# Second attention: scores by two row tiles of 64 rows with four masked heads each, instead of four row tiles of 32 rows with two

## The reference

```python
# x: 64 images x 64 tokens x 256; H = 16 heads of HD = 16
cq = gelu(x @ wq + bq);  ckv = gelu(x @ wkv + bkv)
q_c = cq @ wqc + bqc;    q_r = rope(x @ wqr + bqr)
k_c = ckv @ wkc + bkc;   k_r = rope(x @ wkr + bkr)
v = ckv @ wv + bv
q = gelu(concat(q_c, q_r));  k = gelu(concat(k_c, k_r))    # 256 columns, split in 16 heads
scores = q @ k.T / sqrt(16), causal, in each image and head
out = softmax(scores) @ v @ wo + bo
```

## Time and profile before

| what | us |
|---|---|
| three timed runs | 1585.34, 1585.96, 1579.11 (median 1585.34) |
| the profiled execution, its own time | 1588.56 |
| its span in the trace | 1586.7 |
| TensorE busy | 1388.1 (87% of the span) |
| VectorE busy | 1047.5 (66%) |
| ScalarE busy | 758.5 (48%) |
| GpSimd busy | 634.1 (40%) |
| mean granted clock of TensorE | 0.926 of full speed |

### The profile page before, as it was taken

The page is one execution under the profiler, slowest core; times in us unless marked ns, Lnnn a source line. Parts: engine busy times, 40 slices in busy tenths (PEclk is TensorE's granted clock), DMA queues, the critical chain, the costliest instruction groups (busy, mean ns, idle before and its releaser), DMA issues. The chain is left out here.

```text
span 1586.7 us, 37038 instructions
## 1 busy us (share of the span) xinstructions
PE 1388.1 (87%) x14188; PEld 1219.2 (77%) x14188; DVE 1047.5 (66%) x2196; ACT 758.5 (48%) x1288; POOL 634.1 (40%) x608
## 2 busy tenths in 40 slices
PE   6979999999999987768994588889976889999995
PEld 5867888888888877768994466667756889999994
DVE  4744674674674675876566567888776876666775
ACT  5433444444444442334553366767742346666641
POOL 4005422112112002535627255333336757663765
PEclk9999999999999998889997788999975899999997
DMA  8304664243353104225865000000008248888963
GB/s 287 119 26 152 220 210 147 88 160 116 105 174 134 55 2 156 103 96 172 250 196 161 6 28 28 2 1 2 2 1 318 104 163 253 266 273 255 280 214 111
DMA packets 142883, 215.57 MB, mean 136 GB/s; under 512 B 14336, under 2 KB 112768, under 8 KB 141824
## 3 DMA queue, kind: packets, MB, share of 16 engines
q1 hardware_dynamic: 121648, 160.20, 30.4%
q0 software_dynamic: 18624, 52.45, 10.5%
q10 hardware_dynamic: 2448, 0.61, 0.2%
HBM read 103.64 MB, written 109.58 MB: 134 GB/s over the span
## 5 line engine op out<-in xcount | busy, mean ns | idle before, releaser
L125 PE MATMUL e_p_gu<-e_w_hi,e_xt_hi 128*128 (+1 forms) x676 | 200.8, 297 | 12.9 <-DVE e_xt_lo L723 9.6
L125 PE MATMUL e_p_gu<-e_w_hi,e_xt_lo 128*128 (+1 forms) x676 | 195.0, 288 | 0.0
L125 PE MATMUL e_p_gu<-e_w_lo,e_xt_hi 128*128 (+1 forms) x676 | 194.9, 288 | 0.0
L125 PEld LDWEIGHTS e_p_gu<-e_w_hi,e_xt_hi 128*128 128x128 f32 x676 | 132.9, 197 | 15.1 <-issue 12.8
L1271 POOL DMA_INDIRECT e_xn<-results,e_row_of x112 | 115.6, 1032 | 62.6 <-issue 28.9
L125 PEld LDWEIGHTS e_p_gu<-e_w_lo,e_xt_hi 128*128 128x128 f32 x676 | 133.3, 197 | 0.0
L125 PEld LDWEIGHTS e_p_gu<-e_w_hi,e_xt_lo 128*128 128x128 f32 x676 | 133.2, 197 | 0.0
L125 PE MATMUL e_p_y<-e_w_hi,e_hid_hi 128*128 (+1 forms) x338 | 110.9, 328 | 8.9 <-DVE e_hid_lo L742 7.0
L1254 POOL DMA_INDIRECT rows<-e_xn,e_row_of x96 | 95.5, 995 | 52.9 <-issue 28.7
L1938 DVE TENSOR_TENSOR a_ot_lo<-a_O,a_ot_hi 128x1024 fp32r<-128x1024 f32 x32 | 39.1, 1223 | 115.3 <-ACT a_ot_hi L1881 115.3
L125 PE MATMUL a_J<-a_xt_hi,w_qk_hi 128*128 128x512 f32 x256 | 106.6, 417 | 8.3 <-DVE a_xt_lo L1956 6.3
(11 more groups left out here) (335 smaller groups left out, 4374.4 us busy)
## 6 DMA issues: line engine op xcount, KB each, us to landing
e_moved<-rows SPq DMA_DIRECT2D x121, 256.0 KB, 3.2
results<-e_y SPq DMA_DIRECT2D x121, 256.0 KB
rows<-a_zero SPq DMA_DIRECT2D x28, 1024.0 KB, 5.8
pa_x<-in_x SPq DMA_DIRECT2D x7, 1536.0 KB, 6.5
w_qk_in<-in_we SPq DMA_DIRECT2D x24, 384.0 KB, 6.3
we_parts<-w_qk_in SPq DMA_DIRECT2D x24, 384.0 KB, 2.5
we_parts<-a_e_lo SPq DMA_DIRECT2D x24, 384.0 KB, 2.4
e_w_hi<-we_parts SPq DMA_DIRECT2D x4, 1536.0 KB, 16.1
```

The source lines that it names most:

```text
L125: mm = eng.matmul(out, lhs[a], rhs[b], start=start and n == 0, stop=stop and n == len(terms) - 1, skip_group_check=skip)
```

## The change

A row tile now covers 64 rows, four heads, and there are two of them, one for each PSUM bank. `kz` holds four masked copies of k instead of two (each with every fourth head), so a matmul streams 4 x 64 = 256 columns. A chunk has 8 matmuls instead of 16. No two row tiles share a bank, so the wait on `row_tile` inside the chunk goes, and one increment per chunk is left. `head_mask` and `kc_bias` have four columns instead of two. ScalarE writes four copies where it wrote two, in both places of `queries_keys`. The place of a head in the scores (`scored`) follows.

```diff
+QUAD = 4
-        kz = [sb(f"kz{i}", [P, KD, IMG_T, 2, SEQ]) for i in range(2)]
+        kz = [sb(f"kz{i}", [P, KD, IMG_T, QUAD, SEQ]) for i in range(2)]
-        scored = lambda b, q: 4 * (q % 2) + 2 * (q // 2) + b
+        scored = lambda b, q: 4 * (q // 2) + 2 * b + q % 2
...
                 act.activation(qt[u][:, 1, :], rope[0][:], ACT.Gelu)
-                for head in range(2):
+                for head in range(QUAD):
                     done = act.activation(kz[u][:, 1, :, head, :], by_image(rope[2][:]), ACT.Gelu, scale=head_mask[:, head:head + 1])
...
                 j.wait_full(act, n, KC)
-                for head in range(2):
+                for head in range(QUAD):
                     done = act.activation(kz[u][:, 0, :, head, :], by_image(p_j[:, 0, :]), ACT.Gelu,
                                           scale=head_mask[:, head:head + 1], bias=kc_bias[:, head:head + 1])
...
-                dve.wait_ge(row_tile, 4 * g + 4)
+                dve.wait_ge(row_tile, g + 1)
...
-                for q in range(4):
-                    rows, bank = slice(32 * q, 32 * q + 32), q % 2
-                    if q >= 2:
-                        pe.wait_ge(row_tile, 4 * g + q - 1)
-                    for b in range(KD):
-                        for i in range(2):
-                            img, at = 2 * c + i, (scored(b, q) % 4) * P
-                            mm = pe.matmul(p_s[SEQ * i:SEQ * (i + 1), bank, at:at + P], qt[u][rows, b, img * SEQ:(img + 1) * SEQ],
+                for b in range(KD):
+                    for i in range(2):
+                        img = 2 * c + i
+                        for bank in range(2):
+                            rows = slice(64 * bank, 64 * bank + 64)
+                            mm = pe.matmul(p_s[SEQ * i:SEQ * (i + 1), bank, b * QUAD * SEQ:(b + 1) * QUAD * SEQ],
+                                           qt[u][rows, b, img * SEQ:(img + 1) * SEQ],
                                            kz[u][rows, b, img].rearrange("p a k -> p (a k)"), start=False, stop=True, skip_group_check=True)
-                    mm.then_inc(row_tile, 1)
+                mm.then_inc(row_tile, 1)
```

More of the change, by code:

```diff
@@ L2171, in attention1_phase @@
         st = sb("st", [P, CH, DVE_BN])
-        cos, sin, head_mask = sb("cos", [P, SEQ]), sb("sin", [P, SEQ]), sb("head_mask", [P, 2])
+        cos, sin, head_mask = sb("cos", [P, SEQ]), sb("sin", [P, SEQ]), sb("head_mask", [P, QUAD])
         bias = sb("bias", [P, 9])
-        kc_bias = sb("kc_bias", [P, 2])
+        kc_bias = sb("kc_bias", [P, QUAD])
         bo = sb("bo", [P, D])
@@ L2716, in pack_attention1 @@
     cos, sin = rope_tables()
-    odd = (np.arange(P) // DK1) % 2
+    place = (np.arange(P) // DK1) % QUAD
     return dict(wa1=np.ascontiguousarray(flat.reshape(P, 4, 1024).transpose(1, 0, 2)), bias1=np.ascontiguousarray(bias),
                 bo=w["bo"].reshape(1, D), cos=cos, sin=sin,
-                head_mask=np.stack([1 - odd, odd], axis=1).astype(np.float32))
+                head_mask=np.stack([place == head for head in range(QUAD)], axis=1).astype(np.float32))
 def combine1(c, entry):
```

## The result

The changed kernel takes 1598.35 us (median of four runs, 1596.19 to 1599.04) against 1582.49 us before in the same runs: a ratio of 1.0103, 95% interval [1.0074, 1.0133], or about 16 us slower. Forecast were 13.6 us more, and 1599 us for the whole. The profiled execution took 1596.19 us, with a span of 1594.3 us.

The account below looks back on a forecast made before the run. A ring of waits through all engines was taken as the bound. Delays of 14.8 us, less 3.7 for score blocks, plus 2.5 for the clock, gave 13.6 us more: 1599 us from a 1585.34 us median, range 1588 to 1610.

Parts of the forecast that it names:

- The ring, and ScalarE's copies in it: In tiles n = 3 to 7, waits circle through all engines; copies delay each tile 2.55 us, 12.75 us together.
- hidden by TensorE: Rival: TensorE bounds the tile, ScalarE's free time takes the copies, all score blocks count; -11.8 us, 1574 us; chance 0.07.
- partly hidden: Rival: half of ScalarE's 14.8 us delay is made up within the tile; +1.5 us, 1587 us; chance 0.15.
- The two tiles with gathers: In tiles n = 1 and 2, GpSimd's gathers hide the copies: cost nothing, up to 5.1 us if gathers ended sooner.
- The score block: TensorE's score block shortens from 1.47 to 1.10 us, a gain of 0.37 us (0.28 to 0.45).
- rival 4: Row tiles of 64 rows do not overlap: score block about 1.95 us, 22 us slower, 1607 us; chance 0.05.
- only one block of four counts in a tile: Only `scores(g+2)` gains in each tile; with the very first and last blocks, 10 x 0.37 = 3.7 us saved.
- The term for the clock: TensorE drops to half clock in about half of tiles n = 3 to 7, 1 us each; 2.5 us together.
- 36 or more where the clock falls: Expected tile length in us with a half-clock stretch, against about 34.5 us in other changed tiles.
- the rival with a fall in every tile at 3 us each: Half clock in all five tiles n = 3 to 7, 15 us instead of 2.5: 26 us slower, 1611 us; chance 0.15.
- rival 2: The rival also called "partly hidden": +1.5 us, 1587 us; chance 0.15.
- The start and the end of the phase: Copies delay the second V place before the first tile 2.0 us; the very first and last score blocks save 0.37 each.

Follow-up runs that it names:

- acts_only_filled: Kernel before with ScalarE's four copies and 32-row blocks, first V place computed three times over in tiles n = 3 to 7: ratio 1.0122.
- gap_filled: Changed kernel with TensorE computing the first V place three times over in tiles n = 3 to 7: ratio 1.0079.
- acts_in_slack: Kernel before with four added activations per tile placed where ScalarE waits anyway, written to an unread buffer: ratio 1.0009.
- acts_only: Kernel before, 32-row score blocks kept, with ScalarE writing each half of k four times instead of twice: ratio 1.011.
- scores_only: Changed kernel with 64-row score blocks, ScalarE writing only two of four masked copies, the others zeroed once at the start: ratio 1.000.
- wait_back: Changed kernel with a wait put back between the two halves of each score block: 1597.69 us in one run.

## Why the prediction was right

**The ring, and ScalarE's copies in it.** Right, to 0.1 us in the tiles 5 and 6, where it could be measured alone. `a_ot_hi` came 2.55 us later after the rope sum, the value from the starts of the earlier trace rows; acts_only_filled put the tile at 34.9 us, gap_filled at 34.5. That the place and not the amount of work costs was shown by acts_in_slack. The rival "hidden by TensorE" forecast the opposite of acts_only and is out, and so is "partly hidden", since the whole 2.55 us stayed in the tile.

**The two tiles with gathers.** Right. Tile 1 took 34.87 us and tile 2 37.76; scores_only, the same kernel without the added copies, had 34.85 and 37.77. So the copies cost nothing there.

**The score block.** 1.09 us, forecast 1.10. Row tiles of 64 rows run side by side as the earlier trace rows said, so rival 4 is out. The Trainium skill's other reading (TensorEngine Tiling (Array Packing), Theoretical Speedup: a height of 64 rows for up to 2x, of 32 for up to 4x) would have made the new block the slower one, and the trace disagrees: with two banks the four tiles of 32 rows gained nothing over two of 64 (1.47 against 1.09 us). That only one block of four counts in a tile was right too (0.36 us in scores_only).

**The number, and the clock.** The sum said 13.6 us, and the runs 15.9, with an interval from about 12 to 21: the forecast lies inside it, and no term is shown to be responsible for the 2.3 us. That 1599 came within 1 us of the measured 1598.35 is in part luck. The prediction started from a median of 1585.34 us, and the kernel before had 1582.49 beside the changed one; these 2.85 us made up for the 2.3 that the difference was short by.

The term for the clock (a half-clock stretch in about half of the five tiles, at 1 us each, 2.5 together) was wrong in both of its factors, in opposite directions. The stretches were more: four tiles of five had one behind the two gaps. Their price was lower: 1.00 and 0.46 us in tiles 5 and 6 and nothing in tile 4, 1.5 us in three tiles; those of tile 3 and of the last tile could not be told apart from what stood there without the gaps. The sign "36 or more where the clock falls" was too high for tiles 5 and 6, with 35.5 and 35.0 us, and the rival with a fall in every tile at 3 us each had the count nearly right and the price at least three times too high.

In acts_only the stretch in tiles 5 and 6 was twice as long and cost 2.7 us in each; I had not foreseen that the two halves of the change meet in this way. The new blocks are worth 0.4 us a tile by themselves, and 2.0 and 2.6 us in tiles 5 and 6 once the copies are there. What made the stretch longer is open: wait_back, with blocks of 1.41 us, had stretches of 3.4 us.

Two slips in the chances change nothing here: rival 2 with a tenth of the forecast is 0.21 already and not 0.19, and rival 2's own time, 1587 us, lies just below the stated range.

**The start and the end of the phase** I can't settle to better than 2 us. The first tile took 36.16 us against 32.98 and 35.21 in the two traces of before, the end 44.97 against 41.27 and 44.23; my terms for them were 1.3 us (2.0 less two blocks) and 1.8 us (2.55 less two blocks). How much of the difference is the clock's chance was not tried.

## What to carry to other kernels

Look at who waits for an engine at the very place where work is added, not at how busy it is: ScalarE had 23% of the tile free, and in the tiles without gathers each added microsecond still came through in full, while as much work 14 us later in the tile cost nothing. When half as many matmuls need twice as many operand copies, price the copies at the start-to-start distance of the rows and put what frees a buffer first. And a new gap on TensorE can cost more than its own length, since it may bring the clock down behind it.

## What the runs showed of the hardware

- Two gaps of TensorE of 0.56 and 1.70 us within 3 us of time were followed by 3.4 us at 1.2 GHz in four tiles of five of the changed kernel. In acts_only the same gaps were followed by 3.4 us in tile 3, by 6.8 us in tiles 5, 6 and 7, and by none in tile 4. With the second gap cut to 0.25 us there was no half clock between 1025.0 and 1171.8 us. One gap of 2.07 us alone had brought none.
- Matmuls whose result is written over and never used made a tile shorter, from 35.49 to 34.49 us.
- Four fp32 matmuls at four places of the array: 1024 columns a place took 1.16 us in 16 rounds of 64, and 1.09 us in 4 rounds of 256. A semaphore wait between two halves on TensorE itself cost 0.32 us.
